# Neighbourhood scores over all 128 rows of the array, with zeroed rows for the other heads and no filler ahead of them

## Time and profile before

| | |
|---|---|
| median of 3 runs | 618.61 us (616.03, 618.61, 623.86) |
| span of the profiled execution | 618.9 us (the page gives no other time for it) |
| busy: PE, DVE, ACT, POOL | 89%, 66%, 51%, 8% of the span |
| chain of work that ended last | PE 79%, DVE 10%, issue 7%, ACT 2%, POOL 1% |
| mean granted clock of TensorE | 0.941 |
| first and last score matmul of the stage | 25.0 and 146.4 us |

### The profile page before, as it was taken

How to read it: one execution, slowest core, us unless ns; L and a number is a source line. 1 busy time by engine, 2 the same in 40 slices (tenths; PEclk the granted TensorE clock), 3 DMA queues, 4 the chain that set the end, 5 groups by cost and what they waited for, 6 DMA issues and landing times.

```text
span 618.9 us, 10888 instructions
## 1 busy us (share of the span) xinstructions
PE 548.8 (89%) x4271; PEld 282.6 (46%) x4272; DVE 406.4 (66%) x740; ACT 313.2 (51%) x456; POOL 51.1 (8%) x106
## 2 busy tenths in 40 slices
PE   6999998998589999999999999999999833699962
PEld 5554654564134445444444454444444410266621
DVE  5545557467676656876887687776663457798753
ACT  2644445655036575555655556555656433465440
POOL 6030233212101000010000000000000000000000
PEclk9999999899669999999999999999999957899976
DMA  5000000000000000000000000000000000000001
GB/s 113 1 2 1 2 3 1 0 2 2 1 1 0 1 1 1 2 1 2 2 0 1 1 2 1 2 9 2 1 1 1 0 4 6 10 1 1 2 0 34
DMA packets 9513, 3.32 MB, mean 5 GB/s; under 512 B 8820, under 2 KB 9079, under 8 KB 9463
## 3 DMA queue, kind: packets, MB, share of 16 engines
q1 hardware_dynamic: 8182, 2.61, 1.9%
q10 hardware_dynamic: 1281, 0.01, 0.1%
HBM read 2.09 MB, written 0.52 MB: 4 GB/s over the span
## 4 chain that ended last, share of the span: by engine, by line
PE 79%; DVE 10%; issue 7%; ACT 2%; POOL 1%; POOLq 0%; DVEq 0%; ACTq 0%
PE PS L758 18%; PE PS L781 17%; PE PS L742 10%; PE PS L666 4%; PE PS L680 3%; PE PS L693 3%; PE PS L725 2%; PE PS L517 2%; PE PS L797 2%; PE PS L489 2%; PE PS L985 2%; PE PS L501 2%; PE PS L707 2%; DVE most L1547 2%; PE PS L563 2%
## 5 line engine op out<-in xcount | busy, mean ns | idle before, releaser
L1547 DVE TENSOR_REDUCE most<-PS 128x2 f32<-128x1024 f32 x128 | 156.6, 1224 | 76.7 <-PE PS L742 75.9
L1184 ACT ACTIVATE PT<-PS 128x1024 f32<-128x1024 f32 x128 | 131.0, 1024 | 98.7 <-PE PS L758 98.3
L758 PE MATMUL PS<-qS,aS 128*64 128x512 f16 x1024 | 133.9, 383 | 0.0
L781 PE MATMUL PS<-PT,V 128*64 128x512 f32 x512 | 130.8, 592 | 0.0
L742 PE MATMUL PS<-aS,qS 128*64 128x512 f16 x512 | 80.5, 395 | 10.6 <-DVE most L1547 10.4
L758 PEld LDWEIGHTS PS<-qS,aS 128*64 128x64 f16 x1024 | 56.7, 111 | 62.9 <-issue 28.2
L1140 ACT ACTIVATE prob<-sbias,negm 128x320 f32<-128x320 f32 (+1 forms) x64 | 34.3, 538 | 44.1 <-DVE negm L1593 43.8
L742 PEld LDWEIGHTS PS<-aS,qS 128*64 128x64 f16 x512 | 28.6, 112 | 42.0 <-DVE most L1547 18.5
L781 PEld LDWEIGHTS PS<-PT,V 128*64 128x64 f32 x512 | 36.0, 137 | 23.5 <-issue 0.9
L666 PE MATMUL PS<-ident 128*128 128x256 f16 x128 | 39.1, 306 | 7.3 <-DVE negm L1593 6.4
L1303 POOL TENSOR_TENSOR rstd<-var,minus_half 128x8 f32<-128x8 f32 (+1 forms) x9 | 13.5, 1505 | 357.8 <-DVE var L1411 357.8
(11 more groups left out here) (192 smaller groups left out, 670.5 us busy)
## 6 DMA issues: line engine op xcount, KB each, us to landing
xall<-in_x_dram SPq DMA_DIRECT2D x2, 256.0 KB, 4.4
out_dram<-x SPq DMA_DIRECT2D x4, 128.0 KB, 2.1
w<-in_L_attn_Wq_dram SPq DMA_DIRECT2D x2, 128.0 KB, 2.6
w<-in_L_attn_Wk_dram SPq DMA_DIRECT2D x2, 128.0 KB, 2.8
w<-in_L_attn_Wv_dram SPq DMA_DIRECT2D x2, 128.0 KB, 2.7
fc<-in_L_conv_fc_w_dram SPq DMA_DIRECT2D x2, 64.0 KB, 2.5
wu<-in_L_attn_Wu_dram SPq DMA_DIRECT2D x2, 64.0 KB, 2.4
w1s<-in_L_ffn_ffn_w_dram SPq DMA_DIRECT2D x2, 64.0 KB, 2.1
```

The costliest lines, as they stand in the source:

```text
L758: mm = pe.matmul(PS[h0:h0 + C, score_banks(t) + lane, :], aS[:, k0 + h0:k0 + h0 + C], qS[:, part, lane, toks], start=(part == 0), stop=(pa ...
L781: mm = pe.matmul(PS[cols, 6 + g % 2, :], V[:, img * NT + kt, cols], PT[:, g % 2, lane, kt, :], start=(kt == 0), stop=(kt == NT - 1))
L1184: act.activation(PT[:, g % 2, :, phase, :], PS[:, b0:b0 + 2, :], ACT.Exp).then_inc(c1["exped"], 1)
L1547: dve.tensor_reduce(most[:, g % 2, u // 2, u % 2, :], PS[:, 2:4, :], AX.X, ALU.max, negate=True)\
```

## The change

Each head's queries are now spread out over a tile of their own: `q0M[img]` has, for every head, all 128 partitions, of which only the head's 32 hold queries and the other 96 are zero. The score matmuls take `q0M[img][:, h, part]` and all 128 partitions of `k0S`; the products of the other heads' keys with the zeroes add nothing. To fill it:

- GpSimd sets `q0M[0]` to zero ahead of `power(2)` and `q0M[1]` behind it, both ahead of `wu1`: 4,096 columns of 4 bytes on 128 partitions each.
- SyncE, behind its loads, waits for the zeroes and for the low part of the image's queries, and issues four transfers an image, one a head, 32 partitions by 4 KB, from `q0S` to `q0M` in SBUF. The first unit of an image waits for the four of them and for the drains of its keys.

The filler ahead of the scores is gone; the one ahead of the transposes stays. To make room, `q0M[0]` is laid over `qS`, `q0S` over `kS` and `OT0` over a part of `OT`; only `q0M1` is new.

```diff
--- before.py
+++ after.py
@@ -169,9 +169,8 @@
         xb = sb("xb", [P, B * NT, C])
 
 
-        q0S = sb("q0S", [P, B, 2, TOK], F16)
+        q0M1 = sb("q0M1", [P, NH0, 2, TOK], F16)
         k0S = sb("k0S", [P, B, TOK], F16)
-        OT0 = sb("OT0", [P, 2, P])
 
         aS = sb("aS", [P, B * TOK], F16)
         wT0 = sb("wT0", [P, 3, 2 * NPAIR])
@@ -188,11 +187,14 @@
         V = sb("V", [P, B * NT, P])
         PT = sb("PT", [P, 2, 2, NT, BLK])
         OT = sb("OT", [P, 2, BLK])
+        OT0 = OT[:, :, 0:P]
 
 
 
         qS = sb("qS", [P, 2, 2, B * TOK], F16)
         kS = sb("kS", [P, 2, B * TOK], F16)
+        q0S = kS[:, :, :].rearrange("p i (n t) -> p i n t", n=2)
+        q0M = [qS[:, :, :, :].rearrange("p a l (n t) -> p (a l) n t", n=2), q0M1]
         weight = sb("weight", [P, 2, QT, 2])
         yw = sb("yw", [P, QT, 2, C])
 
@@ -278,6 +280,8 @@
         side_drained = {"act": sem("side_drained_by_scalar"), "dve": sem("side_drained_by_vector")}
         side_high = sem("side_high_made")
         low_rows_made = sem("low_rows_made")
+        heads_cleared = sem("nat_heads_cleared")
+        heads_spread = [sem(f"nat_heads_spread_{img}") for img in range(B)]
         ln_chain = sem("ln_chain")
         normed = sem("normed")
         biased = sem("nat_residual_biased")
@@ -671,14 +675,13 @@
                 first, rows, kind = window_keys(t)
                 if u >= 2:
                     pe.wait_ge(c0["biased"], u - 1)
-                if u == UN0 // B:
-                    side_wait(pe, ("k", 1, 0))
-                    side_wait(pe, ("k", 1, 1))
-                keep_busy(PS[:, u % 2, :])
-                hr = slice(32 * h, 32 * h + 32)
+                if u % (UN0 // B) == 0:
+                    side_wait(pe, ("k", img, 0))
+                    side_wait(pe, ("k", img, 1))
+                    pe.wait_ge(heads_spread[img], 16 * NH0)
                 for part in range(2):
-                    mm = pe.matmul(PS[:, u % 2, 0:rows * WW], q0S[hr, img, part, t * P:(t + 1) * P],
-                                   k0S[hr, img, first * WW:(first + rows) * WW],
+                    mm = pe.matmul(PS[:, u % 2, 0:rows * WW], q0M[img][:, h, part, t * P:(t + 1) * P],
+                                   k0S[:, img, first * WW:(first + rows) * WW],
                                    start=(part == 0), stop=(part == 1))
                 mm.then_inc(c0["scored"], 1)
 
@@ -1307,7 +1310,11 @@
             link(pool.memset(V0[:, :, :, :, HD0:HD0 + 1], 1.0))
             link(pool.memset(prob[:, 0:3, WIN * WW:3 * P], 0.0))
             pool.sem_inc(consts_made, 1)
-            power(2)
+            for img in range(B):
+                if img:
+                    power(2)
+                link(pool.memset(q0M[img][:, :, :, :].rearrange("p h l t -> p (h l t)").bitcast(F32), 0.0))
+                pool.sem_inc(heads_cleared, 1)
             link(pool.memset(wu1[:, :, :, :], 0.0))
             for lane in range(2):
                 link(pool.memset(wu1[C * lane:C * lane + 1, :, lane, C:], 1.0 / KEYC))
@@ -1897,6 +1904,13 @@
                              a["L1_attn_Wu"].rearrange("(n l p) c -> l p n c", l=2, p=C)[lane])\
                   .then_inc(weights_loaded, 16)
 
+            for img in range(B):
+                sp.wait_ge(heads_cleared, img + 1)
+                side_wait(sp, ("q", img, 1))
+                for h in range(NH0):
+                    hr = slice(32 * h, 32 * h + 32)
+                    sp.dma_start(q0M[img][hr, h, :, :], q0S[hr, img, :, :]).then_inc(heads_spread[img], 16)
+
             def of(step, slot):
 
                 n = sp.value_load(control[0:1, bass.ds(slot, 1), 1:2], min_val=0, max_val=NOPS - 1)
```

## The result

The changed kernel takes 597.91 us (median of 4 runs, 596.76 to 599.43) against 619.51 for the kernel before beside it (4 runs); ratio 0.968, 95% interval 0.964 to 0.973 (the ratios leave out runs in a kernel's slower state, so they are not exactly those of the medians). That is faster, as forecast, but by 21.6 us where the forecast of 604 had 14.6: at the low end of its range, 598 to 613, and as a plain median 0.1 us under it. A second, later measurement gave 599.14 against 620.75, ratio 0.967 (0.962 to 0.972). The profiled span is 596.7 against 618.9: 22.2 us less.

The account below looks back on a forecast made before the run. TensorE's own queue was taken to set the pace in most of the neighbourhood attention stage. 618.9 - 12.0 (shorter units) + 0.4 (start) = 607.3, less 3.5 (earlier clock rise) = 603.8, rounded to 604 us; range 598 to 613.

Parts of the forecast that it names:

- the memset that was to cost nothing: Image 0's zeroing on idle GpSimd, 13.2 to 16.8 us, was to end before the queries are ready at 19.8.
- part 1: Neighbourhood scores on TensorE: a full-width pair takes 0.30 us, saving 0.28 a full-clock unit, 20.8 us gross.
- part 2: Neighbourhood attention: waits for VectorE and ScalarE take back 8.8 of the 20.8 us, leaving 12.0.
- one unit's saving lost at each projection: Every fourth unit, a projection makes TensorE wait for VectorE: 11 places lose 0.28 us each, 3.1 us.
- part 4: TensorE's clock rises near 34 us instead of 46.2, gaining 3.5 us.
- rival 3: Neighbourhood stage: earlier clock rise and no fall at 105.3 us, giving 601 us; chance 0.13.
- part 3: Start of the stage: eight transfers and two memsets delay the first score, costing 0.4 us.
- case 1: The forecast itself: the clock rises earlier in the neighbourhood stage, 604 us (600 to 607); chance 0.40.
- Rival 2: Neighbourhood stage: the clock's history stays unchanged, giving 607 us (604 to 610); chance 0.27.
- Rival 4: Neighbourhood stage: VectorE's order, late transfers or another clock fall hide the gain, 611 to 616 us; chance 0.15.
- Rival 5: Without the filler the clock falls early and stays at 1.2 GHz from 46.2 to 150 us: 656 us; chance 0.05.

Follow-up runs that it names:

- the repair of the start: Two variants of the changed kernel: a semaphore for each head's transfer, 598.22 us; image 0's zeroes written by ScalarE instead of GpSimd, 597.09 us.

## Why the prediction was right, and where its sizes were off

**The mechanism held in its main steps.** TensorE's queue set the pace, its shortening carried the gain, VectorE's waits took a part back, the clock rose earlier; the memset that was to cost nothing did not hold. The forecast's direction and case were right; its size, 15.1 us of span, was short of the 22.2 by 7.1. By the table 3.2 us of that lie between units 12 and 44, 2.7 between 44 and 48, 0.6 before unit 12 and 0.6 behind the stage. Term by term:

- **Price of a full-width score (part 1):** 0.27 us, not 0.30, so 0.31 saved a full-clock unit and not 0.28: 1.5 us more over 50 units. The filler's row, 256 columns in 0.12, was scaled up with the columns; the pair takes 0.11 for 256. At half clock the pair takes 0.53 (29.89 to 30.42, with the shape unchanged) rather than 0.48, so a little less was saved there.
- **What VectorE takes back (part 2), the mis-sized step:** charged with 8.8 us. The waits for `negm` grew by 6.2 (6.4 to 12.6). The forecast in its last section said "about 13" for this wait, and its own sum charged more than that growth. Between units 12 and 44, 32 units at 0.31 are 9.9 us gross; 7.5 arrived, so 2.4 were lost where I had 4.7. The rule of one unit's saving lost at each projection did not hold everywhere. From projection to projection

```profile
90.43 0.60 PE L716 MATMUL PS<-pw,OT 128*128 128x260 f32 x2
...
95.85 0.60 PE L716 MATMUL PS<-pw,OT 128*128 128x260 f32 x2
...
101.43 0.60 PE L716 MATMUL PS<-pw,OT 128*128 128x260 f32 x2
```

```profile
77.47 0.60 PE L719 MATMUL PS<-pw,OT 128*128 128x260 f32 x2
...
81.67 0.60 PE L719 MATMUL PS<-pw,OT 128*128 128x260 f32 x2
...
86.31 0.60 PE L719 MATMUL PS<-pw,OT 128*128 128x260 f32 x2
```

  the first period (before, then after) went from 5.42 to 4.20, the saving of all four units, the second from 5.58 to 4.64, three of them, as the rule has it. I had read the rule off one place, 138.37, which lies inside the last layer norm's stretch, where VectorE is at its fullest. That last stretch came out as charged: 2.2 us from unit 48 to 63, as forecast.
- **The clock's rise (part 4):** near 34 was assumed, 31 measured (29.2 in the second execution); the first twelve units gained 7.7 net against 7.1, with the later start, below, working against it. The prediction's 46.2 for the old rise was a unit too early: it was 47. The experiments say what the forecast could only bound: rise at 42.5 to 47 us in all three kernels with 32-row scores, with no, one or two fillers; 39 to 40 with 64 rows; 28 to 33 in all ten profiled executions with 128-row scores, with filler or without, with shape changes or without. The Trainium skill's rule ("TensorE: Matmul & The Clock Gate", Part 1) that the gate goes by how busy TensorE has been is not enough here: before the change TensorE was busy for 21.55 of 21.60 us at half clock, after it for 4.87 of the 6.80 us ahead of the rise. What was in the queue mattered more than that it was full. Why the rows matter to the clock no run shows.
- **The fall at 105.3:** kept in the forecast (rival 3 had it gone, at 601). In the profiled execution it was gone, 2.7 us more from unit 44 to 48 than forecast; in the second execution it was back, near 91, but for 3.4 us instead of 6.8, and those four units still took 6.81 us against 9.44 before. So 1.3 of the 2.7 are one execution's luck; the rest goes with the shorter fall, which no term of the forecast had. The medians of both measurements gain 21.6 us, 0.6 less than the profiled execution.
- **The start (part 3):** 0.4 us behind 24.65, the earliest start without the filler, was forecast; 26.21 is 1.6 behind it. The transfers took 3.32 us to issue, 0.83 each instead of 0.62 (0.62 to 0.83 over the versions), landed 2.9 us after issue (median), and could only be issued at 20.97 and not at 19.8, since GpSimd's memset, called free because GpSimd was idle, held VectorE's copies up for 2.3 us, ahead of the queries' low parts.

**The rivals.** Rival 3 (early rise and no fall, 601) is what the first profiled execution showed, and its 2.5 to 3 us fit the 2.7 above; the second execution had a fall, as case 1 has it. Rival 2 (the clock's history unchanged) is refuted by every full-width kernel. Rival 4 (the gain hidden) does not hold for the change; something like it holds for the repair of the start. Rival 5 (no clock without a filler) is refuted most plainly by the kernel with no filler at all, the second fastest measured.

**Open:** why the scores' rows matter to the clock, and what decides whether a long wait is followed by a fall. Not tried: a wait shortened in VectorE's order rather than covered with fillers. Behind the stage the try scores still take 28.8 us (29.7 before) between the last neighbourhood score and the first global one, some 13 of them at half clock (mean 0.77; 0.73 before); no experiment touched them.

## What to carry to other kernels

When small-row matmuls alternate with full-width ones on TensorE, count the changes of array shape before the rows: a contraction padded with zeroes to the full array can be cheaper than the small one, here 0.27 against 0.38 us for the same columns, and here it brought the clock up where fillers did not. Charge what a second engine takes back by the growth of its waits in the trace, place by place, not by a rule read off its busiest place. And an idle engine's memset is not free before its neighbours' rows have been looked at, one by one: a merged line of four longer copies hid one that stood still.

## What was not expected of the hardware

- Each change of array shape costs 0.1 us at full clock: filler to score takes 0.20 where the score is on 32 rows and 0.11 to 0.13 where both are on 128, and a pair of scores takes 0.38 to the next filler on 32 rows, 0.37 on 64, 0.27 on 128. A matmul of 8 columns on 32 rows between full-width ones costs 0.2 us, with the two changes around it.
- GpSimd's memset of 4,096 columns (3.51 us) kept its pace, and the VectorE copy that began during it (32x896, 0.62 us alone) took 2.95 and ended 0.5 us after it. Image 1's memset, at 35.66, had VectorE's bias steps (0.48) and a copy out of PSUM (0.56) beside it, and they kept their lengths.
- The granted clock reads 1.00 from the start of every trace, while matmuls run at half speed until the first rise (0.74 and 0.45 us for the same pair, 29.89 and 31.62).
- The same kernel, twice profiled, fell to half clock near 91 us in one execution and not in the other; a fall lasted 3.4 us with full-width scores, 6.8 with scores on 32 rows and, once, 27 on 64 rows.
